# One block for the load of x and the first similarity of a four-layer graph kernel

## The reference, cut to what is computed

```python
def _ada_gcn(xn, weight, bias):                      # xn = x transposed to (512, 64, 128)
    x_norm = xn / max(norm(xn, axis=-1), 1e-12)
    mean_sim = einsum('nbl,mbl->nm', x_norm, x_norm) / B
    ...                                              # keep the 153 largest of each row, scale by degrees
    xw = einsum('nbl,lo->nbo', xn, weight)
    return einsum('sd,sbl->dbl', An, xw) + bias
x = layernorm(x + L0(x, adj, bias0))                 # _ada_gcn
x = layernorm(x + L1(x, adj, adj, bias1))            # (adj*adj) applied to each token
x = layernorm(x + L2(x, adj, W_lang, W_grav, W_V, W_O, gate, log_sigma))
x = layernorm(x + L3(x, adj, bias3))                 # _ada_gcn again
```

## Time and profile before

| | us |
|---|---|
| median of 3 runs | 1420.84 |
| lowest and highest | 1418.08, 1422.65 |
| the profiled execution: own time | 1420.99 |
| the profiled execution: span of the core | 1419.3 |
| TensorE busy in the span | 1313.2 (93%) |
| VectorE, ScalarE, GpSimd busy | 1081.6, 818.8, 566.3 |
| first matmul of a gram in the first layer | at 69.72 |

### The profile page before, as it was taken

One profiled execution on the slowest core, in us unless ns is written; L12 is line 12 of the kernel. 1 busy time (PEld: TensorE's weight loads), 2 busy tenths in 40 slices (PEclk: granted clock), 3 DMA queues, 4 the chain that ended last, 5 costly groups with the idle time before them and its releaser, 6 DMA issues. The chain is left out here.

```text
span 1419.3 us, 29584 instructions
## 1 busy us (share of the span) xinstructions
PE 1313.2 (93%) x8776; PEld 726.5 (51%) x8806; DVE 1081.6 (76%) x2169; ACT 818.8 (58%) x1366; POOL 566.3 (40%) x866
## 2 busy tenths in 40 slices
PE   6689988999999889999999999999947997999997
PEld 2156555555555345555555555555514567455553
DVE  0498777888888847888888888888788988356664
ACT  5634345787777633555555555555445446477776
POOL 2100114787787711222222222222222001688887
PEclk9999987999999889999999999999988998999999
DMA  8756200000000022112211111222205440122222
GB/s 325 266 189 210 89 0 1 1 0 0 0 0 0 12 49 38 38 38 38 38 37 37 37 37 37 43 39 39 36 13 177 161 136 1 45 90 81 81 81 97
DMA packets 122971, 93.62 MB, mean 66 GB/s; under 512 B 87712, under 2 KB 87840, under 8 KB 122912
## 3 DMA queue, kind: packets, MB, share of 16 engines
q1 hardware_dynamic: 122720, 92.81, 22.7%
q0 software_dynamic: 192, 0.08, 0.0%
HBM read 54.86 MB, written 17.04 MB: 51 GB/s over the span
## 5 line engine op out<-in xcount | busy, mean ns | idle before, releaser
L546 PE MATMUL pair<-unit_lo,unit_hi 128*128 128x512 f16 x512 | 178.8, 386 | 29.5 <-ACT unit_hi L617 24.7
L2030 POOL TENSOR_TENSOR sq_lo<-sq,sq_hi 128x512 f16<-128x512 f32 x60 | 69.6, 1160 | 139.2 <-ACT sq_hi L1803 139.2
L550 PE MATMUL diag<-unit_hi 128*128 128x128 f16 x512 | 113.4, 221 | 0.0
L548 PE MATMUL pair<-unit_hi 128*128 128x384 f16 (+2 forms) x384 | 106.4, 277 | 0.0
L1150 PE MATMUL po<-an_h,xwh 128*128 128x512 f16 x256 | 98.0, 383 | 0.0
L1151 PE MATMUL po<-an_l,xwh 128*128 128x512 f16 x256 | 97.9, 382 | 0.0
L1152 PE MATMUL po<-an_h,xwl 128*128 128x512 f16 x256 | 97.8, 382 | 0.0
L1785 PE MATMUL work<-m_h,xT 128*128 128x512 f16 x256 | 97.0, 379 | 0.0
L1786 PE MATMUL work<-m_l,xT 128*128 128x512 f16 x256 | 97.0, 379 | 0.0
L1787 PE MATMUL work<-m_h,xT 128*128 128x512 f16 x256 | 97.0, 379 | 0.0
L1089 POOL TENSOR_TENSOR x_all<-x_all,t 128x512 f32 (+1 forms) x64 | 81.2, 1269 | 16.8 <-ACT t L983 12.1
(11 more groups left out here) (438 smaller groups left out, 4237.7 us busy)
## 6 DMA issues: line engine op xcount, KB each, us to landing
x_all<-in_x_dram SPq DMA_DIRECT2D x16, 1024.0 KB, 14.5
tl<-rn_rows SPq DMA_DIRECT2D x64, 256.0 KB, 3.7
sim<-rn_rows SPq DMA_DIRECT2D x64, 256.0 KB, 3.7
out_dram<-x_all SPq DMA_DIRECT2D x64, 256.0 KB, 2.0
weights_a<-in_L_gnn_W_lang_dram SPq DMA_DIRECT2D x1, 1024.0 KB, 11.4
weights_b<-in_L_gnn_W_grav_dram SPq DMA_DIRECT2D x1, 1024.0 KB, 8.3
weights_a<-in_L_gnn_W_O_dram SPq DMA_DIRECT2D x1, 1024.0 KB, 10.6
an_h<-in_L_gnn_W_V_dram SPq DMA_DIRECT2D x1, 512.0 KB, 5.6
```

What stands on the lines that cost most here:

```text
L546: nc.tensor.matmul(pair[i][:], stat, lo[:, r, :], start=first, stop=False, skip_group_check=True)
L548: nc.tensor.matmul(pair[i][:, (i + 1) * P:], stat, hi[:, r, (i + 1) * P:], start=False, stop=final, skip_group_check=True)
L550: last = nc.tensor.matmul(diag[:, i * P:(i + 1) * P], stat, stat, start=(first and i == 0), stop=final, skip_group_check=True)
```

## The change

The two blocks of the first layer become one, `load_and_compare`. The similarity is written as a class that both layers use; in the last layer the order of instructions on each engine stays as it was. In the new block:

- no block end and no meeting of all engines lies between load and similarity;
- SyncE goes from the store of the early norms, and the wait for it, straight to the broadcast loads; W_O is loaded in four pieces of 256 KB behind the batches at rows 8, 12, 16 and 20; W_V stays after row 31; W_grav comes behind the batch at row 44;
- of the rows from 24 on, every fourth (27, 31, ... 63: ten rows) is squared by GpSimd, into a ring of two tiles of its own; the ring of ScalarE lies in the buffer of W_grav;
- ScalarE takes the early root at q = 9 instead of q = 10, and behind it makes the high part of the W_lang product straight from PSUM (seven instructions); VectorE makes the low part straight from PSUM behind `refine` (seven instructions); the scaled copy and GpSimd's low part are gone;
- the W_lang product lies in the banks `pair`, so TensorE waits for its low part before the first gram;
- behind its squares ScalarE goes on with the casts, and GpSimd with the late store; VectorE waits for all 64 sums only ahead of the late clamp, behind the first batch.

```diff
-    def during_load(self, ctx):
-        self.arrive("wl")
-        self.lang = Operand(self.k, self, 0, "wl", *packed([self.k.ps(ctx, f"u{i}") for i in range(3)]))
+    def during_load(self, banks):
+        self.arrive("wl", "wg", "wo", "wv")
+        self.lang = Operand(self.k, self, 0, "wl", *packed(banks[0:3]))
...
+    SHARED = range(6, PARTS)
     with ExitStack() as ctx:
-        sq = k.sb(ctx, "sq", [P, RS, N])
+        sq = mix.b
+        sq_own = k.sb(ctx, "sq_pool", [P, 2, N])
...
+        def on_pool(b):
+            return b // per in SHARED and b % per == per - 1
+        def free(b):
+            earlier = [i for i in range(b) if on_pool(i) == on_pool(b)]
+            ring = 2 if on_pool(b) else RS
+            return earlier[-ring] + 1 if len(earlier) >= ring else 0
...
                 early.store(sp)
                 early.all_stored(sp)
+                for base in range(0, B // 2, R):
+                    sim.load(sp, base)
+                    if base == 2 * R:
+                        sp.wait_ge(mix.lang.lo_r, 2 * C - 1)
+                    if 2 * R <= base < 6 * R:
+                        mix.load_rows(sp, "wo", mix.a, base // R - 2)
+                sim.late.all_stored(sp)
+                mix.load_value_weights(sp, ops)
+                with strided(sp, B // 2, B // 2 + 4 * R, R) as base:
+                    sim.load(sp, base)
+                sp.wait_ge(sums, B)
+                mix.load(sp, "wg", mix.b)
+                with strided(sp, B // 2 + 4 * R, B, R) as base:
+                    sim.load(sp, base)
...
                 tokens.on_pool(k, pool, w2_r, b1_in)
-                mix.lang.scales(pool)
-                mix.lang.lo_part(pool, mix.a)
+                for b in range(B):
+                    if b == 9 * per:
+                        mix.lang.scales(pool)
+                    if on_pool(b):
+                        pool.wait_ge(x_in[b // per], 16)
+                        need(pool, sums, free(b))
+                        pool.tensor_tensor(made(b)[2], k.X[:, b, :], k.X[:, b, :], ALU.mult).then_inc(sq_pool, 1)
+                sim.late.store(pool)
+                pool.wait_ge(early.top, 1)
+                sim.greatest(pool)
...
-                    if q == PARTS // 2 + 2:
+                    if q == PARTS // 2 + 1:
                         early.take_root(act)
+                        mix.lang.hi_direct(act)
                     act.wait_ge(x_in[q], 16)
...
+                for r in range(R):
+                    sim.take_hi(act, 0, r, True)
+                sim.late.take_root(act)
+                with strided(act, R, B, R) as base:
+                    for r in range(R):
+                        sim.take_hi(act, base, r)
...
-                    pe.wait_ge(sq_ready, b + 1)
+                    pe.wait_ge(*made(b)[0:2])
...
+                pe.wait_ge(mix.lang.lo_r, 2 * C - 1)
+                pe.wait_ge(mix.lang.q_in, 1)
+                for r in range(R):
+                    sim.gram(pe, 0, r, r == 0, False)
...
                 early.refine(dve)
-                mix.lang.scale_and_hi_on_vector(dve, mix.a)
+                mix.lang.lo_direct(dve)
+                sim.units(dve, 0, True)
+                dve.wait_ge(sums, B)
+                sim.late.clamp(dve)
+                sim.units(dve, R)
+                sim.late.invert(dve)
+                sim.units(dve, 2 * R)
+                sim.late.refine(dve)
+                with strided(dve, 3 * R, B, R) as base:
+                    sim.units(dve, base)
```

More of the change, by code:

```diff
@@ L509, in _ @@
             def _(sp):
[L510 to L528, removed]
+                sim.load(sp, 0)
+                with strided(sp, R, sim.split, R) as base:
+                    sim.load(sp, base)
@@ L530, in _ @@
+                sim.late.all_stored(sp)
+                with strided(sp, sim.split, B, R) as base:
+                    sim.load(sp, base)
             @block.gpsimd
             def _(pool):
[L532 to L537, removed]
+                last.scales(pool)
@@ L539, in _ @@
+                last.low_parts(pool)
+                sim.late.store(pool)
+                sim.greatest(pool)
             @block.tensor
             def _(pe):
[L541 to L551, removed]
-                    last.then_inc(gram_done, 1)
@@ L611, in _ @@
+                dve.wait_ge(last.sums, 1)
+                sim.late.clamp(dve)
+                sim.units(dve, 6 * R)
+                sim.late.invert(dve)
+                sim.units(dve, 7 * R)
+                sim.late.refine(dve)
+                with strided(dve, 8 * R, B, R) as base:
+                    sim.units(dve, base)
+                sim.weights(dve, ops, ahead)
             @block.scalar
             def _(act):
-                def split(b, r, start):
-                    act.wait_ge(unit_ready, b + 1)
-                    if not start:
-                        act.wait_ge(gram_done, b - R + 1)
-                    nc.scalar.activation(hi[:, r, :], unit[:, r, :], ACT.Copy).then_inc(hi_ready, 1)
@@ L634, in _, with split @@
-                late.take_root(act)
-                with strided(act, head, B, R) as base:
+                def split(first, end):
+                    for b in range(first, end):
+                        sim.take_hi(act, b // R * R, b % R, b < R)
+                split(0, 3 * R)
+                last.normalise(act)
+                split(3 * R, 4 * R)
+                last.squares(act, range(0, 2))
+                split(4 * R, 4 * R + 2)
+                last.squares(act, range(2, G))
+                split(4 * R + 2, 6 * R)
@@ L1615, in scratch_tiles @@
     return h[:, 0:N], h[:, N:2 * N], l[:, 0:N]
-def select_neighbours(k, rows_bank, scale, layer, mix, ops, ahead=None, last=None):
-    with ExitStack() as banks:
-        pair, diag = similarity(k, banks, rows_bank, scale, layer, mix, ops, ahead, last)
-        neighbours(k, pair, diag, rows_bank, ops, mix, ahead)
 def kernel_mix(k, w, rows_bank, head):
@@ L2089, in build @@
             ahead = EarlyProjections(k, layer)
-            select_neighbours(k, rows_bank, S_SQ, 3, None, ops, ahead=ahead, last=LastGroup(k, layer, ahead))
+            last = LastGroup(k, layer, ahead)
+            with ExitStack() as banks:
+                pair, diag = similarity(k, banks, rows_bank, S_SQ, ops, ahead, last)
+                neighbours(k, pair, diag, rows_bank, ops, None, ahead)
             propagate(k, ops, k.bias3, out, ahead)
```

243 lines of the change are left out of this document (129 added, 114 removed).

## The result

The kernel after takes 1415.08 us (median of 10 runs, 1413.23 to 1416.95), the kernel before 1422.65 in the same comparison. The ratio is 0.9952, with a 95% interval from 0.9942 to 0.9962, that is 5.4 to 8.3 us faster; 7.5 us had been forecast. The forecast time itself, 1413.3, was counted from the first median of before, 1420.84, so its difference is what compares. The profiled execution of after took 1413.23 us, the fastest of its ten, 7.8 less than that of before, and its span is 1411.4 against 1419.3.

A forecast was written before the change was run, and what follows sets the result against it. TensorE was taken as the bound from 93.14 us on, VectorE before. Terms: 8.0 won at the block end, 0.5 lost to weights' loads, so 7.5 us won: 1413.3 us by the median; range 1407.5 to 1417.0.

The forecast's parts named there:

- The block end: Between load and similarity: broadcasts wait only for the early norms, landing at 55.0; first gram at 61.7, 8.0 us sooner.
- The store's issue: SyncE's store of the early norms: issued at 47.7 instead of 51.89, landing with the last of x; bounds 51.2 and 55.5.
- The squares: Before the first gram: ScalarE done at 55.8, TensorE at 56.9, hidden by 4.8 us; each us beyond counts in full.
- GpSimd beside VectorE: During refine: GpSimd squares may cost some 0.5 us per meeting, at most 3.8 us; only the store's issue moves.
- The low part on VectorE: Behind refine: seven instructions, at most 4.4 us, done by 52.1 or 56.3, before the first product; costs nothing.
- The weights' loads: W_O between batches costs nothing, up to 0.5 us; W_grav at row 44 is charged +0.5 us, bounds 0 and 1.5.
- The second batch and the clock: After the first gram: TensorE's clock starts at half as before, so VectorE's 1.57 us broadcast wait is not won.
- the rival: At the first gram: the clock is still whole when grams begin, 9.1 us won, 1411.7; chance 0.22.
- The sum: Whole kernel, likeliest: 8.0 - 0.5 = 7.5 us won, 1413.3 us by the median; chance 0.41.
- The fourth broadcast: Rival, first batch: late by itself, landing at 62.4, first gram at 63.8; 5.4 us won, 1415.4; chance 0.14.
- The store did not land early: Rival, early norms: the store does not wait for x, lands at 51.2; 12.8 us won, 1408.0; chance 0.13.
- GpSimd did not hold TensorE up: Rival, the squares: slow GpSimd squares delay TensorE; at 5 us each the kernel takes 1427; chance 0.04.

The follow-up runs named there:

- the run with the weights early: Kernel after, with W_O in four pieces right behind the first four broadcasts and W_grav behind it once the squares are done: 1416.30 us, ratio 0.9965.
- the second execution of after: The kernel after, unchanged, profiled again beside later variants on one chip: median 1414.01 us, ratio 0.9947 to before.

## Why the prediction was right, and where not

- *The block end.* Right, in place and nearly in size: broadcasts at 55.0 foretold, 55.27 measured; first product 58.2 and 58.49; first gram 61.7 and 62.29. The wait put back takes the similarity's end back by 2.8 to 3.5 us.
- *The store's issue.* Foretold at 47.7; in this execution it was 50.21, since the table load began at 42.73 and not at 40.2. In four other executions with the root at q = 9 and ten squares on GpSimd, whose squares ran sooner, 48.1 to 48.5 was reached. It made no difference, as argued: x's end covers it. The reason given, the order in SyncE's queue, did not hold. The lower bound adds up to 51.3 and not 51.2; nothing hangs on it.
- *The squares.* The term was mis-sized: TensorE ended them at 60.04 and not at 56.9, so the cover was 2.25 us and not 4.8. ScalarE began its last squares late, as the table load came 2.5 us later than taken; its 21 last squares took 11.68 us, 0.556 each in place of 0.524 (0.7 us together); and TensorE ended 1.73 us behind ScalarE and not 1.1. In other runs with the same squares the end was 57.96 to 59.88, so 56.9 was at least a us short in each. It could not be reached by the prediction's own figure for x: where ScalarE waited for the last part of x, the squares ended 3.1 to 3.2 us behind its arrival (55.68 and 58.79 in the run with the weights early), so with x at 55.0 they end at 58.1 or later. The sum did not suffer, as the cover held. That the squares are cover and not gain once the wait is gone fits the run without GpSimd's; with the wait in place their end counts.
- *GpSimd beside VectorE.* The three instructions of refine took 0.68 us each as before, so nothing was lost there. The one meeting went against GpSimd: its squares take 1.04 us (1.27 was taken), and one of them 1.20, begun while refine's last instruction ran. The rule of the Trainium skill (SBUF - State Buffer, Who interferes with whom) allows that: who begins first holds the other up. The trace agrees: the two ran together for 50.18 - 49.89 = 0.29 us, and the square took 0.16 us longer.

```profile
49.50 0.68 DVE L217 SCALAR_TENSOR_TENSOR an_l<-an_h,an_l 64x512 f32<-64x512 f32 x1
...
49.89 1.20 POOL L553 TENSOR_TENSOR sq_pool<-x_all 128x512 f32<-128x512 f32 x1 [3.55 <-PE rows_bank L593]
51.60 1.04 POOL L553 TENSOR_TENSOR sq_pool<-x_all 128x512 f32<-128x512 f32 x1 [0.52 <-PE rows_bank L593]
```

- *The low part on VectorE.* Right: it ended at 52.4, under cover until 58.5.
- *The weights' loads.* +0.5 foretold; measured 1.02 - 0.46 = +0.56, but at W_V and not at W_grav, for which VectorE waited 0.71 us without a stop of TensorE. That it fits so well is chance: in the other executions with both loads at these places TensorE's stops added up to anything from none (all squares on ScalarE) to 0.53 at W_V and 1.49 at W_grav (early root at its old place). With 256 KB behind each batch no stop came.
- *The second batch and the clock.* The likeliest case had the half clock at the first gram and none of the 1.57 us won. It came between that and the rival: whole at the start, half from 63.4 for 3.4 us; VectorE waited 0.78 us for the fourth cast, and 8.24 - 7.43 = 0.81 us were won by the row at 84.90. In the second execution of after the likeliest case did come: the clock was half at the first gram, and 23.20 us lay between it and that row, against 23.42 in before and 22.61 here.
- *The sum.* 7.43 + 0.81 - 0.56 = 7.68 at the end of the similarity, against 8.0 + 0 - 0.5 = 7.5. The mechanism is as foretold; that the sum is so close is partly luck, as the first gram was 0.6 us later than forecast and the clock gave back 0.8. In the second execution of after the same mark gives 167.05 - 160.08 = 7.0.
- *The rivals.* The fourth broadcast was not late by itself: without weights behind it the four products run through here, and in other executions one of the later three stood for 0.2 to 0.9 us and not 2.13. The store did not land early. GpSimd did not hold TensorE up.

## What to carry to other kernels

Of a wait at a block's end, count what each engine would do without it, and then ask what is late next: here the waiting gave way to the landing of x. Relief for an engine that only covers something else can turn into idle time of the bound engine, behind which the clock may fall; here that cost 0.8 to 1.0 us, about what the relief had won at the first gram. Moving no work, some or most could not be told apart in the totals. A large transfer issued behind small ones that are already in flight delays them, and pieces that fit into the slack did so far less.

## What the runs showed of the hardware

- The granted clock fell after TensorE had started again: in after it idled 2.25 us up to 62.29, and the clock fell at 63.4; in the run with the store in a queue of its own it idled 2.14 us up to 62.92, and the clock fell at 63.6; with the early root at its old place 3.71 us up to 63.14, and it fell at 64.0. With idle times of 1.85, 1.08, 0.87 and 0.41 us ahead of the first gram it did not fall there. In three of these four executions it fell some 15 us later, at 77.2 to 77.9, behind 2.49 us of idling; after the same 2.49 us at 77.82 in the fourth it did not.
- A store of 64 KB in two transfers, in another queue than 1 MB loads in flight, was reported as landed 4 us after its issue, when the loads had ended.
- ScalarE waited for the last part of x until 54.76, 55.17 and 55.68 in three executions with the same order of instructions up to there, and the squares' end, with the same squares on the same engines, between 57.96 and 60.04.
